# Expert slots of a mixture-of-experts layer: the two bias products taken out of the slot, the biases brought in by ScalarE and by the residual's operation

## The reference

```python
t = xf * lax.rsqrt(mean(xf * xf) + EPS) * norm_w
vals, idx = top_k(t @ gate_w.T + gate_b, 4);  G[token, idx] = softmax(vals)
h = einsum('mh,eoh->emo', t, w1) + b1[:, None, :]
a = minimum(h[..., ::2], 7);  b = clip(h[..., 1::2], -7, 7)
act = a * sigmoid(1.702 * a) * (b + 1)
y = einsum('emi,edi->emd', act, w2) + b2[:, None, :]
return x + einsum('me,emd->md', G, y)
```

## Time and profile before

| | us |
|---|---|
| median of 3 executions | 1021.15 (1018.97 to 1021.18) |
| the profiled execution | 1019.23 |
| its span, first to last instruction | 1017.5 |
| PE busy | 722.9 (71%) |
| DVE busy | 610.9 (60%) |
| ACT busy | 445.6 (44%) |
| POOL busy | 328.3 (32%) |
| granted TensorE clock, mean | 0.903 of 2.4 GHz |

### The profile page before, as it was taken

The page is one execution under the profiler, slowest core; times in us unless marked ns, Lnnn a source line. Parts: engine busy times, 40 slices in busy tenths (PEclk is TensorE's granted clock), DMA queues, the critical chain, the costliest instruction groups (busy, mean ns, idle before and its releaser), DMA issues.

```text
span 1017.5 us, 22304 instructions
## 1 busy us (share of the span) xinstructions
PE 722.9 (71%) x5722; PEld 428.6 (42%) x5722; DVE 610.9 (60%) x1961; ACT 445.6 (44%) x974; POOL 328.3 (32%) x356
## 2 busy tenths in 40 slices
PE   2222079999899917778889488487129999999930
PEld 2111046666565613223343243244116666666620
DVE  6778235666555564787787368347305666665647
ACT  2534035555555524357465235261015555555510
POOL 3667713333333314101111600605512333333320
PEclk9999999999999966889999788797559999999975
DMA  9754345555444253631201313315333333333148
GB/s 311 261 212 161 136 118 167 168 168 169 131 136 127 76 176 93 197 116 49 80 18 53 132 45 130 131 44 202 118 106 99 98 99 101 95 96 91 50 133 280
DMA packets 120111, 131.63 MB, mean 129 GB/s; under 512 B 39596, under 2 KB 101525, under 8 KB 119864
## 3 DMA queue, kind: packets, MB, share of 16 engines
q1 hardware_dynamic: 101656, 91.11, 29.9%
q0 software_dynamic: 13728, 34.64, 9.5%
q10 hardware_dynamic: 4608, 4.46, 1.2%
HBM read 69.54 MB, written 64.21 MB: 131 GB/s over the span
## 4 chain that ended last, share of the span: by engine, by line
PE 44%; SPq 14%; DVE 13%; issue 13%; ACT 5%; another core or an unknown queue 5%; ACTq 3%; DMA 3%; DVEq 0%; POOLq 0%; POOL 0%
PE banks L407 13%; PE banks L429 6%; SPq L218 3%; ACT w2s L1434 3%; SPq L232 3%; SPq L217 2%; PE banks L1211 2%; PE banks L1165 2%; DVE X L727 2%; SPq L230 2%; PE banks L1277 2%; PE banks L1235 2%; PE banks L403 2%; PE banks L416 2%
## 5 line engine op out<-in xcount | busy, mean ns | idle before, releaser
L341 POOL DMA_INDIRECT y_rows<-y,goal x158 | 155.6, 985 | 318.5 <-ACT y L499 296.0
L407 PE MATMUL banks<-w1s,rT 128*128 x948 | 233.7, 383 | 0.0
L689 DVE TENSOR_SCALAR pbh<-banks 128x256 f32<-128x256 f32 x158 | 67.1, 425 | 197.3 <-ACT pbh L485 125.9
L1597 DVE CUSTOM_DVE_ANT_0 pbh<-banks,maskq 128x128 bf16<-128x128 f32 (+3 forms) x256 | 114.0, 487 | 77.8 <-PE banks L1188 46.3
L1434 ACT ACTIVATE w2s<-banks 128x1024 f32<-128x1024 f32 (+3 forms) x128 | 89.7, 701 | 123.4 <-PE banks L1219 84.3
L407 PEld LDWEIGHTS banks<-w1s,rT 128*128 128x128 f16 x948 | 93.7, 99 | 97.2 <-issue 4.0
L429 PE MATMUL banks<-w2s,hsT 128*128 x948 | 129.2, 273 | 0.0
L478 ACT ACTIVATE rT<-banks 128x512 f16<-128x512 f16 x158 | 93.5, 593 | 42.7 <-issue 34.7
L485 ACT ACTIVATE pbh<-banks 128x256 f32<-128x256 f32 x158 | 60.5, 383 | 117.3 <-PE banks L407 113.9
L1125 POOL DMA_INDIRECT x_rows<-row,row_to x64 | 61.7, 964 | 121.8 <-DVE row_to L1731 103.5
L389 PE MATMUL banks<-ident,row 128*128 128x128 f16 x632 | 62.6, 223 | 51.2 <-DMA goal<-x_rows 50.4
(11 more groups left out here) (238 smaller groups left out, 1059.7 us busy)
## 6 DMA issues: line engine op xcount, KB each, us to landing
row<-x_rows SPq DMA_DIRECT2D x158, 128.0 KB
arena<-in_w SPq DMA_DIRECT2D x16, 512.0 KB, 7.1
w1s<-y_rows SPq DMA_DIRECT2D x16, 512.0 KB, 4.7
arena<-y_rows SPq DMA_DIRECT2D x16, 512.0 KB, 7.8
qk_split<-w1s SPq DMA_DIRECT2D x48, 128.0 KB
arena<-qk_split SPq DMA_DIRECT2D x64, 96.0 KB, 2.3
w_lent<-w1s SPq DMA_DIRECT2D x22, 256.0 KB
w1s<-w_lent SPq DMA_DIRECT2D x11, 512.0 KB
```

The source lines that it names most:

```text
L341: pool.indirect_dma_start(y_rows[m], bass.IndirectOffsetOnAxis(ap=goal[:, n % NG, :], axis=0), y[:, n % NY, :], None, bounds_check=K * T - ...
L407: mm = pe.matmul(o, rT[:, n % 2, 2 * r + k, :], w1s[:, bass.ds(e, 1), k, w, :], start=False, stop=(k == HC - 1 and w == 1))
L689: dve.tensor_scalar(b[:, n % 2, :], bank[2 + n % 2][:, INNER:], (LIMIT + 1.0) * S, (1.0 - LIMIT) * S, ALU.min, ALU.max).then_inc(each("b"), 1)
L1597: dve.tensor_tensor_reduce(junk[:, (n * U + j) % 3, 0:W], query_bank[(n * U + j) % 3][:, 0:W], maskq[:, SEQ - W:], 1.0, -3e38, ALU.add, AL ...
```

## The change

1. `up(n)` loses its bias matmul. Scaled `b1` goes once to DRAM (`b1_rows`, 16 x 512) and from there to all 128 partitions of SBUF, 4.2 MB in six DMAs (`up_bias`, in the arena where the weights were staged). In layer 0 SP issues them in `load_up_bias`: two ahead of the slot table, one each after `load_rows` of n = 4 to 7; in layer 1 all six follow the return of the lent `w2` weights near the end of attention. Per slot ACT copies the expert's row block into the PSUM bank (`up_bias_in`), after `clip_b` has read the bank's last content, and the six matmuls accumulate on it. ACT therefore needs the slot's expert: one more value load per slot, on ACT.
2. `down(n)` loses its bias matmul. Instead the gates are laid out by expert (`dense`, `by_expert`, 5 short steps of DVE in slots 2 to 6), transposed (`turn_gates`, 4 times per layer, and `byT_out` on ACT) and multiplied with `b2` once for each of the 16 token tiles (`bias_product`, one matmul of 256 columns); the residual's operation adds that product from PSUM in place of `drop`.
3. `y_out` goes to DVE in two slots of three and stays on ACT in the third; the residual falls into slots where ACT has `y_out`, every third slot.
4. On PE `down(s-2)` now stands ahead of `turn_h(s-1)`.
5. SP's early loads for the attention move: the attention weights to n = 72 and 73, the four table-row DMAs to n = 78 behind the wait for the last `up_bias_in`. `combined` semaphores are replaced by waits on `summed`.

```diff
                 def up(n, e):
                     pe.wait_ge(each("rT"), n + 1)
-                    if n >= 2:
-                        pe.wait_ge(each("b"), n - 1)
+                    pe.wait_ge(each("up_bias"), n + 1)
...
-                    pe.matmul(o, pick[:, bass.ds(e, 1), :].rearrange("p o n -> p (o n)"), bias[:, 0:2 * INNER],
-                              start=True, stop=False)
                     for k in range(HC):
...
                 def down(n, e):
                     pe.wait_ge(each("hT"), n + 1)
                     if n >= 2:
-                        pe.wait_ge(each("y"), n - 1)
+                        pe.wait_ge(*y_done(n - 2))
                     o = bank[6 + n % 2][:, 0:H]
-                    pe.matmul(o, pick[:, bass.ds(e, 1), :].rearrange("p o n -> p (o n)"), bias[:, 2 * INNER:],
-                              start=True, stop=False)
...
+                def bias_product(s, i):
+                    pe.wait_ge(each("rT"), s + 2)
+                    pe.wait_ge(each("byT"), m * B + i // TPB + 1)
+                    pe.matmul(bank[(s + 1) % 2][:, 0:H], byT[0:PARTS, i // TPB % 2, i % TPB * P:(i % TPB + 1) * P],
+                              b2_parts[0:PARTS, :], start=True, stop=True).then_inc(each("bias_made"), 1)
...
+                def up_bias_in(n, e):
+                    if n - FIRST < E and (n - FIRST) % GROUP == 0:
+                        r = (n - FIRST) // GROUP
+                        act.wait_ge(stage_loaded[r], weights_in(r) * 32 + m * 16 + 16)
+                    if n < FIRST + 2:
+                        act.wait_ge(each("banks_written"), m * 2 + 2)
+                    else:
+                        act.wait_ge(each("b"), n - 1)
+                    act.activation(bank[2 + n % 2], up_bias[:, bass.ds(e, 1), :].rearrange("p o n -> p (o n)"),
+                                   ACT.Copy).then_inc(each("up_bias"), 1)
...
                     if s + 2 < LAST:
                         rows_out(s + 2)
+                        up_bias_in(s + 2, held[s + 2])
+                    if s + 3 < LAST:
+                        held[s + 3] = expert(s + 3)
...
                     if s < LAST:
                         h_hi(s)
-                    if s >= FIRST + 2:
+                    if s >= FIRST + 2 and by_act(s - 2):
                         y_out(s - 2)
...
+                def residual(s, i):
+                    dve.wait_ge(each("bias_made"), m * NT + i + 1)
+                    dve.scalar_tensor_tensor(X[:, i, :], X[:, i, :], grow[:, i:i + 1], bank[(s + 1) % 2][:, 0:H], ALU.mult,
+                                             ALU.add).then_inc(each("residual"), 1)
...
-                if n in (62, 63):
-                    sp.dma_start(w_raw[:, n - 62, :], wqkv[:, n - 62, :]).then_inc(s("w_loaded"), 16)
+                if n == 72:
+                    sp.wait_ge(sem("slot_bias_made"), NT)
+                if n in (72, 73):
+                    sp.dma_start(w_raw[:, n - 72, :], wqkv[:, n - 72, :]).then_inc(s("w_loaded"), 16)
```

More of the change, by code:

```diff
@@ L100, in build @@
         w2s = keep("w2s", [P, E, 2, 2, H], f16)
-        bias = keep("bias", [P, 2 * INNER + H], f16)
-        pick = keep("pick", [P, E, P], f16)
+        b1_rows = nc.dram_tensor("b1_rows", (E, 2 * INNER), f32, kind="Internal").ap()
+        b2_parts = keep("b2_parts", [P, H], f16)
+        dense = keep("dense", [P, NT, E])
+        by_expert = keep("by_expert", [P, NT, PARTS], f16)
         ones16 = keep("ones16", [P, P], f16)
@@ L282, in store_out @@
                 def store_out(j):
-                    sp.wait_ge(ev("combined"), j + 1)
+                    sp.wait_ge(ev("summed"), (j + 1) * K * 2)
                     sp.dma_start(out[j * 2 * P:(j + 1) * 2 * P, :].rearrange("(t p) h -> p t h", p=P),
@@ L291, in sync @@
                         if i >= NB:
-                            sp.wait_ge(ev("combined"), (i - NB) // 2 + 1)
+                            sp.wait_ge(ev("summed"), ((i - NB) // 2 + 1) * K * 2)
                         load_back(i)
@@ L387, in turn_rows @@
                         pe.wait_ge(each("rT"), n - 1)
+                    if gates_at(n - 3) is not None:
+                        pe.wait_ge(each("byT"), m * B + gates_at(n - 3) + 1)
+                    if bias_at(n - 3) is not None:
+                        pe.wait_ge(each("residual"), m * NT + bias_at(n - 3) + 1)
                     for q in range(4):
@@ L452, in tensor @@
                     pe.wait_ge(sem("mid_lent_back"), 16 * (E - LENT + 1))
+                for o in (2, 3):
+                    pe.matmul(bank[o], ones16[:, :], ones16[:, :].unsqueeze(1).broadcast_to([P, 4, P]),
+                              start=True, stop=True).then_inc(each("banks_written"), 1)
                 held = {FIRST: expert(FIRST)}
@@ L520, in scalar @@
                         act.wait_ge(route("to_exp"), g + 1)
+                        act.activation(dense[:, g * TPB:(g + 1) * TPB, :], dense[:, g * TPB:(g + 1) * TPB, :], ACT.Exp)
                         act.activation(ex[:, g * TPB:(g + 1) * TPB, :], ex[:, g * TPB:(g + 1) * TPB, :], ACT.Exp)\
@@ L729, in combine @@
                             add.then_inc(ev("summed"), 1)
-                    dve.wait_ge(ev("summed"), (j + 1) * K * 2)
-                    dve.sem_inc(ev("combined"), 1)
                 split = 0 if m == 0 else E
@@ L775, in vector @@
                         h_out(s)
-                    if s > FIRST:
+                    if FIRST <= s - 1 < LAST:
                         hT_out(s - 1)
+                    if s >= FIRST + 2 and not by_act(s - 2):
+                        y_out(s - 2)
+                    if bias_at(s) is not None:
+                        residual(s, bias_at(s))
                     if s < LAST:
                         h_lo(s)
-                    if 24 <= s - FIRST < 24 + 2 * NT and (s - FIRST) % 2 == 0:
-                        residual((s - FIRST - 24) // 2)
+                    if 2 <= s - FIRST < 7:
+                        gates_by_expert(s - FIRST - 2)
                 for j in range(NT // 2 if m == 1 else 0):
@@ L1014, in load_back @@
                     if i >= NK:
-                        sp.wait_ge(s("combined"), (i - NK) // 2 + 1)
+                        sp.wait_ge(s("summed"), ((i - NK) // 2 + 1) * K * 2)
                     src = y_rows[0].rearrange("(k t p) h -> t p k h", k=K, p=P)[i]
@@ L1095, in sync @@
                         sp.wait_ge(s("v"), 2 * B)
-                        sp.wait_ge(s("combined"), NT // 2)
+                        sp.wait_ge(s("summed"), NT * K)
                         sp.wait_ge(s("bo_added"), NT)
@@ L1468, in exps @@
                     act.wait_ge(route("to_exp"), B + b + 1)
+                    act.activation(dense[:, of(b), :], dense[:, of(b), :], ACT.Exp)
                     act.activation(ex[:, of(b), :], ex[:, of(b), :], ACT.Exp).then_inc(route("exps"), 1)
```

190 lines of the change are left out of this document (139 added, 51 removed).

## The result

The changed kernel takes 994.0 us (median of 4, 986.68 to 995.64) against 1021.16 us (median of 4, 1018.97 to 1022.03). The ratio is 0.9724, with a 95% interval of 0.969 to 0.9757. The profiled execution took 995.64 us, its span is 993.6 us.

A forecast was written before the change was run, and what follows sets the result against it. PE was taken to bound layer 1 (2.72 us per slot) and SP's row issues layer 0 (3.11 us). Gains of 21.6 in layer 1 and 5.5 in layer 0, less 0.4, make 26.7 us: 994 us, range 984 to 1008.

The forecast's parts named there:

- PE bounds layer 1, 0.32 us per slot: Layer 1: without two bias products PE's turn falls from 2.72 to 2.40 us; net gain 21.6 us.
- SP holds layer 0: Layer 0: SP issues rows every 3.11 us per slot, slower than PE, so PE waits for rows from about half on.
- layer 0's term: Layer 0: gain about 5.5 us of the 25.3 the products promise, with rows of n = 78 transposed at 344.9.
- ACT's load hidden beside the copy: Each slot on ACT: value load runs beside `up_bias_in`, `h_hi` starts at g + 1.6 (g: start of `gelu`); cost zero.
- The circle of the rival: ACT, load not overlapping the copy: loop of 2.62 us against PE's 2.40, gain 13 us, time 1007; chance 13%.
- Start and the rest: Layer starts: up to 3.2 us later on ACT at no cost; `up_bias` transfer zero; `dense` operations cost 0.4 us.
- Sum: Whole kernel: 21.6 + 5.5 - 0.4 = 26.7 us less, giving 992.5 or 994.4; 994 taken.
- The clock rival: Layer 0: PE 77% busy, clock falls to 0.85, costing 6.7 us behind n = 62, time 1001; chance 8%.
- The rule on value loads: ACT, each slot: the skill's 600 ns floor would make a load about 0.9 us; without overlap, a 2.9 us loop, layer 1 loses.

The follow-up runs named there:

- pe_back: Changed kernel with two idle products, of 512 and 256 columns, put back on PE in every `down`: 1021.67 us, ratio 0.9993 to the kernel before.
- pool_after: Changed kernel with the 48 further DMAs of layer 0's slots n = 14 to 61 issued by POOL instead of SP: 968.72 us, ratio 0.9472 to before.
- sp_more: Changed kernel with one more SP DMA per slot in layer 1, n = 14 to 61, to an unread scratch tensor: 959.17 us, ratio 0.993, second chip.
- act_load2: Changed kernel with ACT's value load made twice in every slot, second result unused: 1009.17 us, ratio 0.9862 to the kernel before.

## Why the prediction was right, and where it was not

The forecast was 994 us, the median is 994.0. The sum behind it was not as exact as that; the steps one by one:

- *PE bounds layer 1, 0.32 us per slot:* right. The turn is 2.40 us, pe_back takes the whole gain away. The layer gave 22.6 us where 21.6 were forecast.
- *SP holds layer 0:* right in kind, and shown from both sides by pool_after and sp_more. The size of the term was off: 5.5 us forecast, 0.8 measured.
- *Where layer 0's term was mis-sized:* the rows of n = 78 were to be transposed at 344.9 and were at 349.93, 5.0 us later, which is no gain on the 349.88 of before. The parts: SP issued n = 14 at 156.29, 2.0 us after the forecast's 154.3 (1.4 us because its first rows went out at 125.44 instead of 124.07, 0.2 because the four turns with `up_bias` loads took 2.88 us against 2.16 before, 0.72 more and not 0.67). SP's stretch from n = 14 to 62 took 305.17 - 156.29 = 148.9 us, forecast 149.2. The last 16 turns took 39.5 us instead of 38.5. The largest part is the last: from issue to transposes of n = 78 it took 349.93 - 344.67 = 5.26 us where I had 2.87, 2.4 us more. The mis-sized term is this 2.87, read from one slot, n = 68, and taken as fixed for the end, where the margin was nil.
- *Why the rows were late there:* PE used up its margin at n = 74: it was ready at 338.13, the rows came for 340.34, 4.84 us after their issue at 335.50, and 4 turns of 2.40 were left. The records of the trace show two causes for these 4.84 us. The first packet of these rows went out at 337.03, 1.5 us after the issue, where n = 72 and 76 needed 1.0, and the weights loaded behind n = 73 were under way until 337.10; that is some 0.6 us for the moved loads. Then all but the last of the landing records were in by 338.84 and the last one at 340.29, with a packet of the "instruction" queue from 338.21 to 339.08; that is 1.45 us. Neither was run alone.
- *ACT's load hidden beside the copy:* right; `h_hi` came at g + 1.59, forecast g + 1.6. That the two agree so closely is in part chance: the forecast let the copy end at g + 1.46 and the load 0.14 us later, while the copy began 0.1 us later than forecast and itself ended at g + 1.57. The copy takes 0.60 us, forecast 0.6. The circle of the rival is real; act_load2 lengthened the turns by 0.21 us on average where 0.17 was expected, and had a second circle through `y_out` in it.
- *Start and the rest:* the layer-0 start is 2.4 us later at PE (third transpose 139.15 against 136.80) and costs nothing, as said, though in a kernel relieved of SP's load it probably would (not run). The stage between the layers lost 1.1 us, 0.4 forecast. The end gained 1.6 us, which I had at zero, and it is there in pe_back too, so PE's columns are not the cause. `combine` no longer waits behind each pair; that is the likely cause and was not run alone.
- *Sum:* 26.7 us forecast. The profiled executions differ by 1019.23 - 995.64 = 23.6 us, the medians by 27.2. The exact hit is luck. In the profiles layer 0 fell 4.7 us short, while layer 1 and the end brought 2.6 us more than forecast; and the profiled execution of before lies 1.9 us below its median, that of the changed kernel 1.6 us above. The four executions of the changed kernel span 9 us.
- *The clock rival:* did not happen as priced. Behind n = 62 the granted clock is 1.00, the 2.4 GHz level, and so it is between 245 and 320 us, where PE was busy 65 of 75 us. The rival's share of 77% was not quite reached: 2.40 of the mean turn of 2.96 us is 81%. But the clock did fall once in this layer, to the 1.2 GHz level from 206.4 to 209.8 us, after the wait of 2.77 us; it cost 3.80 - 2.40 = 1.4 us in a stretch that SP's pace holds anyway. The Trainium skill, "TensorE: Matmul & The Clock Gate", section "HAM oscillation — how this bites in real kernels", warns that waits for DMA between bursts of products bring the clock down again and again. This trace shows it once; behind the other 16 waits, of 0.3 to 2.2 us, it shows nothing of the kind.
- *The rule on value loads:* by the Trainium skill, "DMA: Bandwidth & Descriptors", section "Latency and other measured facts", a load takes about 600 ns at least. Here the load itself is 277 ns and the whole read some 0.55 us. The measurement decides.

## What to carry to other kernels

A bound that is read from one stage holds for that stage only: before pricing a saving on the busiest engine, follow each stage's supply (here SP's issues per slot) at the *new* pace. Moving 48 plain DMAs from the engine whose sequencer sets the pace to one with free time was worth 25 us on the changed kernel, about as much as the change itself, but only 12 us on the kernel before, whose PE (2.72 us per slot) was less ahead of SP's pace (3.1); it cost the engine that took them 0.6 us each. A time from issue to landing that is read from one slot is no constant: where the margin is nil, look at its spread. When work is moved onto a second engine, look for the circle of waits it closes, add up its terms, and compare that with the new turn rather than comparing busy shares.

## What the runs showed of the hardware

- A value load on ACT starts while the copy issued ahead of it is still running (820.6 against 820.55 to 821.15, act_load2), and its 0.5 us are hidden as long as the copy lasts 0.6 us.
- One further DMA turns SP's slot from 2.28 into 2.95 us in both layers, whether it carries 256 KB of weights (layer 0) or 136 KB of padding (layer 1 of sp_more, 2.96 us on average). So the price doesn't go by the bytes.
- The rows land 2.3 to 2.7 us after their issue (medians of before, after and pool_after). Single slots take up to 5.1 us, with one record of 32 late and a 16 KB packet of the "instruction" queue just ahead of it (n = 28, 42, 46 and 74 of the changed kernel).
- After a wait of PE of 2.77 us the granted clock was at 1.2 GHz from 206.4 to 209.8 us, and the turn took 3.80 us instead of 2.40.
- Three chips ran the same kernel before in 1022.48, 967.50 and 964.54 us. In the profiles of the changed kernel (993.6 and 935.7 us) the difference lies between the layers (396 and 350 us) and in the way to the slots (139.15 and 122.84 us), while layer 1 took 199 us on both. What makes the difference stays open.
